# Gate and up of the second feed-forward block: eight partial products against seven, batch outside

## The reference, cut to what matters

```
def _L1_ffn_ref(x, w_gate, w_up, w_down):
    gate = jnp.einsum('bsd,hd->bsh', x, w_gate)      # 512 -> 2048
    up = jnp.einsum('bsd,hd->bsh', x, w_up)          # 512 -> 2048
    gated = jax.nn.silu(gate) * up
    return jnp.einsum('bsh,dh->bsd', gated, w_down)  # 2048 -> 512
...
x = x + 0.5 * _L1_ffn_ref(_layernorm(x), ...)
```

## Time and profile before

| | |
|---|---|
| runs | 2634.18, 2636.2, 2642.79 us |
| profiled execution: span from first to last instruction | 2632.3 us |
| TensorE busy | 2535.4 us (96%), mean granted clock 0.992 |
| VectorE / ScalarE / GpSimd busy | 1533.2 (58%) / 1035.6 (39%) / 981.6 us (37%) |
| chain that ended last, by engine | PE 81%, DVE 6%, POOL 2%, ACT 2%, SPq 2% |

### The profile page before, as it was taken

One profiled execution on the slowest core, in us unless ns is written; L12 is line 12 of the kernel. 1 busy time (PEld: TensorE's weight loads), 2 busy tenths in 40 slices (PEclk: granted clock), 3 DMA queues, 4 the chain that ended last, 5 costly groups with the idle time before them and its releaser, 6 DMA issues.

```text
span 2632.3 us, 44135 instructions
## 1 busy us (share of the span) xinstructions
PE 2535.4 (96%) x16928; PEld 2013.0 (76%) x16928; DVE 1533.2 (58%) x3356; ACT 1035.6 (39%) x1885; POOL 981.6 (37%) x1373
## 2 busy tenths in 40 slices
PE   6999989999999999999999999999999999999999
PEld 4788867667668888888888878677776678888887
DVE  7777579979975445433333345798589643333333
ACT  6555346656653223311111133566466431111111
POOL 5333566666643225211111122666366521111110
PEclk9999989999999999999999999999999999999999
DMA  4222131222220110100000002343233100000001
GB/s 148 73 73 73 39 76 46 51 68 64 48 93 1 36 45 12 37 25 25 24 25 25 25 17 58 92 94 75 52 88 79 37 32 25 24 25 25 25 17 64
DMA packets 72002, 128.73 MB, mean 49 GB/s; under 512 B 15728, under 2 KB 24944, under 8 KB 71792
## 3 DMA queue, kind: packets, MB, share of 16 engines
q1 hardware_dynamic: 71792, 125.92, 17.3%
HBM read 62.42 MB, written 13.63 MB: 29 GB/s over the span
## 4 chain that ended last, share of the span: by engine, by line
PE 81%; DVE 6%; POOL 2%; ACT 2%; SPq 2%; issue 2%; DMA 1%; DVEq 0%; ACTq 0%; POOLq 0%
PE psum L1049 65%; PE psum L1167 5%; PE psum L1130 4%; PE psum L1148 4%; PE psum L1178 2%; DVE psum L1501 2%; SPq L1745 1%; PE psum L1058 1%; DVE s1a0rden L1540 1%; ACT s1a0e L1335 1%; SPq L1764 0%; POOL s1a0e L1671 0%; ACT s4a1e L1335 0%; PE psum L1137 0%; POOL rstd L1610 0%
## 5 line engine op out<-in xcount | busy, mean ns | idle before, releaser
L1501 DVE CUSTOM_DVE_ANT_0 psum<-psum,mask_q 128x512 f32<-128x512 f32 (+5 forms) x768 | 413.2, 574 | 101.2 <-PE psum L1130 97.3
L1049 PE MATMUL psum<-hA_hi,wmem 128*128 128x256 f32 (+1 forms) x1536 | 405.2, 334 | 0.5 <-DVE s1a0negmax L1501 0.3
L1049 PEld LDWEIGHTS psum<-hA_hi,wmem 128*128 128x128 f32 x1536 | 270.3, 190 | 31.8 <-DVE s1a0negmax L1501 1.5
L1049 PE MATMUL psum<-hA_lo,wmem 128*128 128x512 f32 (+1 forms) x864 | 293.8, 340 | 0.0
L1335 ACT ACTIVATE s4a1e<-psum,p_scale 128x384 f32<-128x384 f32 (+5 forms) x384 | 205.5, 581 | 95.2 <-PE psum L1148 91.8
L1335 ACT ACTIVATE s1a0e<-psum,p_scale 128x384 f32<-128x384 f32 (+5 forms) x384 | 202.4, 578 | 78.1 <-PE psum L1148 76.8
L1454 DVE SCALAR_TENSOR_TENSOR x<-psum,x 128x512 f32<-128x512 f32 x256 | 175.7, 689 | 97.4 <-PE psum L1049 93.9
L1425 DVE TENSOR_TENSOR s5f1prod<-psum,s5f1silu 128x512 f32<-128x512 f32 x64 | 44.2, 691 | 303.7 <-PE psum L1049 303.7
L1425 DVE TENSOR_TENSOR s3f1prod<-psum,s3f1silu 128x512 f32<-128x512 f32 x64 | 44.2, 691 | 294.2 <-PE psum L1049 294.2
L1635 POOL TENSOR_TENSOR wmem<-raw,wmem 128x512 fp32r<-128x512 f32 x58 | 74.3, 1290 | 315.7 <-ACT wmem L1237 315.7
L1049 PE MATMUL psum<-s3f1w,s3f1a 128*128 128x512 f32 x768 | 181.6, 390 | 0.9 <-POOL s3f1w L1635 0.9
(11 more groups left out here) (195 smaller groups left out, 5581.8 us busy)
## 6 DMA issues: line engine op xcount, KB each, us to landing
s1a0qst<-s1a0qs SPq DMA_DIRECT2D x96, 128.0 KB, 2.3
s4a1qst<-s4a1qs SPq DMA_DIRECT2D x96, 128.0 KB, 2.4
s4a1kst<-s4a1ks SPq DMA_DIRECT2D x96, 128.0 KB, 2.4
raw<-in_gate SPq DMA_DIRECT2D x44, 256.0 KB, 2.9
raw<-in_up SPq DMA_DIRECT2D x44, 256.0 KB, 2.8
raw<-in_down SPq DMA_DIRECT2D x44, 256.0 KB, 2.8
rounded<-s0f0w SPq DMA_DIRECT2D x24, 256.0 KB, 2.0
s2f0w<-rounded SPq DMA_DIRECT2D x24, 256.0 KB, 4.9
```

The costliest lines, as they stand in the source:

```text
L1049: ins = pe.matmul(out_, w, m, start=n == 0, stop=n == len(terms) - 1)
L1501: dve.tensor_tensor_reduce(scores, scores, mask_q[:, first:first + pw], -1.0, -MASKED, ALU.add, ALU.min, T[s]["negmax"][n % 2][:, column:c ...
```

## The change

For f1 the chunk loop is replaced by rounds. A round is one batch (1024 tokens) and one group of 256 hidden columns; 16 rounds are a stage, batch outside, so that every weight group is loaded and split twice. In a round, gate and up are each one product of a 256 x 512 weight block with a 512 x 1024 block of LN output, both cut in 2 x 2. The eight half-depth products are replaced by Winograd's seven (`mul`, i = 0 to 6): 128 hidden columns, depth 256, 512 tokens, 6 matmuls each. They use seven combinations of weight blocks (sums by GpSimd, `g_sum`, split by `g_hi` on ScalarE and `g_lo` on GpSimd) and seven of the LN output, once per batch (`f_copy` on ScalarE and `f_sub` on VectorE per tile, split by `h_hi` and `h_lo`).

Products 0, 2, 4 and 5 accumulate in one PSUM bank, and 3 and 6 in another; product 1 has its own. After products 0, 2 and 4 the partial sum is copied out (`snap`: the gate's by ScalarE, up's by VectorE) before the next product may go on in the bank. VectorE adds copy and bank (`sum`). Then silu, multiplication (`gated`), `ahi`, `alo` as before, and `fold` is the old `down`. A round is 14 `mul` and 8 `fold`, 132 matmuls of 128x512. Round r's folds stand in round r+1.

`TURNS`, `AFTER_TURN` and the rest order this. Core of the diff:

```diff
+OPENS = {0: 0, 1: 1, 2: 0, 3: 3, 4: 0, 5: 0, 6: 3}
+SNAPS = (0, 2, 4)
+
+OUTS = ((0, 0, 1, 0), (1, 1, 3, 4), (1, 0, 5, None), (0, 1, 6, 2))
...
+FOLDS_AT = (2, 3, 4, 5, 6, 8, 9, 10)
+EARLY_TURNS = 8
...
+            for j in turns if r == 0 else range(len(TURNS)):
+                plan.extend(turn(s, r, j))
+                norms.tick(1 if j % 7 == 0 else 0)
+                weights.tick(int(j in (4, 5) or j > DOWN_AT[-1]))
...
+            def mul(s, r, n, i):
...
+                copied = {2: 0, 4: 2, 5: 4}.get(i)
+                if copied is not None:
+                    on.wait_ge(*copy_done(s, r, n, copied))
+                if i == 6:
+                    on.wait_ge(sem["sum"], at("sum", "sum", s, r, n, 1))
+                on.wait_ge(sem["g_lo"], at("g_lo", "g_lo", s, r, n, i))
+                on.wait_ge(sem["h_lo"], at("h_lo", "h_lo", s, r // GROUPS["f1"], i))
+                w = [by_half(part) for part in T[s]["block"][n][i]]
+                h = T[s]["h"][i]
+                terms = [(w[wp][:, k, :], h[hp][:, k, :]) for k in range(2) for wp, hp in THREE]
+                for k, (left, right) in enumerate(terms):
+                    ins = pe.matmul(psum[:, bank, :], left, right, start=OPENS[i] == i and k == 0,
+                                    stop=k == len(terms) - 1, skip_group_check=True)
...
+                dve.tensor_tensor(t1, bank[:, 0:2, :], b11, ALU.subtract).then_inc(sem["f_t1"], 1)
+                dve.tensor_tensor(t3, b22, bank[:, 0:2, :], ALU.subtract).then_inc(sem["f_t3"], 1)
...
+                dve.tensor_tensor(t2, bank[:, 2:4, :], t1, ALU.subtract).then_inc(sem["f_t2"], 1)
...
+                dve.tensor_tensor(t4, b21, t2, ALU.subtract).then_inc(sem["f_t4"], 1)
...
+                on.wait_ge(sem["mul"], at("mul", "mul", s, r, n, i))
+                dve.tensor_copy(T[s]["snap"][n][i == 2][:], psum[:, banks["mul", s, r, n, 0][0], :]).then_inc(sem["snap_up"], 1)
...
+                dve.tensor_tensor(buf[:], psum[:, banks["mul", s, r, n, OPENS[i]][0], :],
+                                  T[s]["snap"][n][copied == 2][:], ALU.add).then_inc(sem["sum"], 1)
...
+                pool.tensor_tensor(sums[:, 0], a21, a22, ALU.add).then_inc(sem["g_s1"], 1)
+                pool.tensor_tensor(sums[:, 2], a11, a21, ALU.subtract).then_inc(sem["g_s3"], 1)
...
+                pool.tensor_tensor(sums[:, 1], sums[:, 0], a11, ALU.subtract).then_inc(sem["g_s2"], 1)
...
+                pool.tensor_tensor(sums[:, 3], a12, sums[:, 1], ALU.subtract).then_inc(sem["g_s4"], 1)
```

More of the change, by code:

```diff
@@ L141, in make_plan, with norm_steps, norm @@
     last_norm, last_weight = {}, {}
[L143 to L146, removed]
+    def norm_steps(s, t):
+        kinds = ["ln_stats", "ln_norm", "ln_tp"]
+        if not by_rounds(s):
+            kinds += ["ln_hi", "ln_lo"]
+        else:
+            kinds += ["f_copy"] + ["f_sub"] * (t // CT % 2)
+        return [(kind, s, t) for kind in kinds]
+    def norm(s, c, into=0):
+        jobs = []
+        for t in range(c * CT, (c + 1) * CT):
+            steps = norm_steps(s, t)
+            wait = [[]] * (by_rounds(s) or by_rounds(s - 1)) * into
+            jobs.append([[steps[0]], *wait, [steps[1]], *wait, *wait, steps[2:]])
         last_norm[s, c] = jobs[-1]
@@ L175, in first_products @@
     def first_products(s):
+        if by_rounds(s):
+            steps = [[("begin", s)] + h_split(s, 0, 2)]
+            turns = [turn(s, 0, j) for j in range(EARLY_TURNS)]
+            return steps + [sum(turns[j:j + 2], []) for j in range(0, EARLY_TURNS, 2)]
         mts = MTS[STAGES[s]]
@@ L340, in attention @@
         put(jobs, last + 2, (UNITS - 4) // len(jobs))
+        if by_rounds(s + 1):
+            for i, at in enumerate(H_EARLY_AT):
+                put([[[step] for step in h_split(s + 1, 0, i)]], last + at, 0)
         if grouped:
@@ L421 @@
     "gu": ("gate", "up", "silu", "prod", "a_hi"), "a_lo": ("a_lo",),
+    "f_copy": ("f_copy",), "f_sub": ("f_t1", "f_t3", "f_t2", "f_t4"), "h_hi": ("h_hi",),
+    "h_lo": ("h_lo",), "g_sum": ("g_s1", "g_s3", "g_s2", "g_s4"), "g_hi": ("g_hi",),
+    "g_lo": ("g_lo",), "mul": ("mul",), "sum": ("sum",), "silu": ("silu_q",),
+    "gated": ("gated",), "ahi": ("ahi",), "alo": ("alo",), "fold": ("fold", "x_add"),
     "k_ones": ("k_ones",),
@@ L435, in raised @@
     if kind == "down":
-        return ("down", "dso", "x_pool") if STAGES[step[1]] == "f0" else ("down", "x_add")
+        return "down", "dso", "x_pool"
+    if kind == "snap":
+        return (("snap",), ("snap_up",))[step[3]]
     if kind == "v_out":
@@ L593, in run, with emptied_by @@
         return done[step]
+def emptied_by(s, r, n, i):
+    if i:
+        return "sum", s, r, n, OUT_OF[i]
+    return "silu" if n == GATE else "gated", s, r, OUT_OF[i]
 def bank_turns(plan):
@@ L867, in w_read @@
             p = s - 1
+            if by_rounds(s) and name == "down":
+                return [(sem["fold"], at("fold", "fold", s, g - 1, ST - 1))] if g else []
             if is_ffn(s):
@@ L1572, in vector_program @@
                      "q8": q8_, "q_b": q_b, "gu": gu, "a_lo": a_lo, "down": down,
+                     "f_sub": f_sub, "h_lo": h_lo, "snap": snap, "sum": sum_, "gated": gated_, "alo": alo, "fold": fold,
                      "turned": turned, "row": row, "row_min": row_min, "m_lo": m_lo, "v_out": v_out,
```

568 lines of the change are left out of this document (482 added, 86 removed).

## The result

The changed kernel took 2565.12 us (median of 4 runs, 2560.02 to 2569.59) against 2636.89 for the kernel before: ratio 0.9722, 95% interval 0.9703 to 0.9742. Its profiled execution took 2567.41 us with a span of 2565.7, against the 2552.2 that the sum gave; 66.6 us went where 80.1 were forecast. The median is 9.0 us over the forecast's 2556.1. The time lies in the stated range and the forecast's direction held; 13.5 us between the two profiled executions are to be accounted for. Ratios leave out two executions in a slower state, one of the kernel before (4170 us) and one of experiment 6 (5720 us).

What follows compares the result with a forecast made beforehand. TensorE's matmul count was taken to bound the f1 stages. Terms -87.2 + 1 + 8.7 - 6.6 + 3 + 0 + 1 = -80.1 took the 2632.3 us span to 2552.2; plus 3.9, 2556.1 us; own range 2546 to 2568, stretched for rivals to 2541 to 2588.

Steps and rivals of the forecast that it cites:

- The bound and the count: Both f1 stages: only the number of matmuls counts, 2304 a stage before and 2112 after, 384 fewer in two stages.
- The price of a matmul: f1 bodies: 0.2272 us each, from 32.71 us for 144 matmuls, so 384 fewer give -87.2 us.
- Added work in a round: Per 30.0 us round: VectorE 17.3, ScalarE 14.1, GpSimd 18.9 us, all under TensorE; +1 us for both stages' middle.
- a round over 30.5 us: Sign of being wrong: a round was to take 30.0 us from one first product to the next.
- Entry of s3: First round of s3: ScalarE and VectorE work exceeds TensorE's 19.1 us, so TensorE waits; +8.7 us, bounds 0 and 17.
- Entry of s5: Start of s5: 4 us lost where 10.6 were lost to waits and low clock; -6.6 us, bounds -10.6 to 0.
- Last group of s4: End of s4: GpSimd gets 6.6 us more work ahead of the exponentials' sums; +3 us, bounds 0 and 6.6.
- From s3 to s4: Stage boundary: LN work leaves it and the attention's first splits start 3 us later; 0, bounds -2 and +2.
- The lock between VectorE and GpSimd: First round of s3: two-SBUF-input VectorE instructions wait for GpSimd, some 2 us in all, 2558 for the sum.
- 1 (entries hide better): Rival: entries of s3 and s5 cost +1 and -8, all else +1; -93.4, 2543 us; chance 0.12.
- 2 (each round loses a product's time): Rival: a late copy or weight split costs 1.36 us every round, 44 us more, 2600; chance 0.15, milder or full.
- 3 (GpSimd the bound): Rival: GpSimd's queue bounds every round at 34.1 us, 45 over before, 2681 us; chance 0.03.

Runs made afterwards that it cites:

- experiment 6: Changed kernel with VectorE's low parts of token blocks done for one column only in the first batch of both f1 stages: 2551.04 us, ratio 0.9678.
- experiment 5: Changed kernel with product 1 of gate and up done twice in every round, giving back the 384 matmuls: 2644.27 us, ratio 1.0030.
- experiment 8: Changed kernel with ScalarE copying up's partial sums as well as the gate's: 2565.7 us, ratio 0.9732.
- experiment 2: Kernel before with feed-forward operand addresses aligned (64 bytes ahead of hA, 128 in s2): 2626.16 us, ratio 0.9956.
- Experiment 7: Changed kernel with GpSimd's low parts of weight blocks done for one column only in the first round of both f1 stages: 2559.41 us, ratio 0.971.
- experiments 1 and 3: Changed kernel with all feed-forward operands at the same address modulo 256: 2550.1 us; changed kernel with all f1 operands 192 bytes apart: 2574.82 us.

## Why the prediction was right, and where it was off

**The bound and the count.** Right. TensorE's waits are 0.3 us in the body of s3 and 1.6 in that of s5, experiment 5 prices 192 matmuls a stage at what they take once the entries are taken off, and experiment 8 shows that 3 x 0.69 us a round can move from VectorE to ScalarE without a change that can be told.

**The price of a matmul** is the term that was mis-sized most. At the measured means a body is 2304 x 0.2286 before and 2112 x 0.2310 after in s3, 2304 x 0.2285 and 2112 x 0.2297 in s5: 79.8 us in place of 87.2 (80.2 by these rounded means), a miss of 7.4. "The same multiplication two chunks later" was one sample in a kernel whose operands change place every two groups, and I carried it over to tiles that the change allots anew. The stretches of the earlier trace rows held a warning: 475.00 us for 2085 matmuls is 0.2278, and 488.00 for 2137 is 0.2284. At equal alignment the change is worth 2626.16 - 2550.1 = 76 us.

**Added work in a round.** The sizes are right where an instruction runs alone: copy 0.69, GpSimd 0.74. GpSimd was busy 63 to 67% of the bodies where 18.9 of 30.0 is 63%. VectorE was busier than forecast, 64 to 65% for 58%: its low parts (L1934) and those multiplications that read SBUF alone (L1927) took 0.88 us in the mean in s3 where 0.69 was put. The prediction had called the instructions with two SBUF inputs too few to matter; for the time they were, since VectorE was not the bound. It also named a round over 30.5 us as a sign of being wrong. From one round's first fold to the next one's it is 30.47 us in s3 with no other work, but 31.4 in the eight rounds of s3 that hold eight transposes of the LN each.

**Entry of s3**, forecast +8.7. The start held (1049.14 for 1049.1), and the waits for blocks came to 7.8 us, with the one for `g_lo`, where the steps of the prediction add up to 8.4. Not counted were the half clock behind the last of them, 3.4 us that cost 1.7, and the down split's 2.0. In all 1.25 + 7.8 + 1.7 + 2.0 - 0.9 = 11.9. I had seen at s5 of before that the clock was down after a wait of 3.75 us, and did not carry it to the waits that I was adding.

**Entry of s5**, forecast -6.6. The waits foreseen as 2.7 and 1.3 us were 2.35 and 2.23; the down split (1.3) and the clock (1.7) came on top: 7.6 lost for 10.6, so -3.0.

**Last group of s4**, forecast +3: from the first exponential of s4 to the last it took 2.0 us longer. That is all of s4, and in experiment 2, which leaves s4's steps as before, the same stretch took 4.5 us more than before, so the +2 is not shown to come from the last group. **From s3 to s4**, forecast 0: the last fold of s3 and the first exponential of s4 are 28.0 and 28.1 us earlier than before, 0.

**The sum** of the misses: 7.4 + 3.2 + 3.6 - 1.0 = 13.2 of 13.5 us. That it comes so close is in part luck. Cut at stage boundaries, the 66.6 us are 28.0 up to s3's last fold, -3.7 from there to s5's first product, and 42.3 in s5, and the terms above miss these by 1 to 2 us each, in both directions. Part of the 13.5 is also the pair of executions: wherever both are on record a time is about 1.7 us over its span, so the span of 2632.3 goes with a time of some 2634.0, next to the fastest run of the kernel before, while the changed kernel's profiled time is 2.3 over its median. The 3.9 us that the prediction added to the span were in part this. By the medians 71.8 us went. The rivals' list holds one slip of 0.2: -87.2 + 1 - 8 + 1 is -93.2, not -93.4.

**The lock between VectorE and GpSimd.** A token block's split (L1894), with two SBUF inputs, in the changed kernel (ns min/median/max):

```profile
L1894 DVE TENSOR_TENSOR s3f1h<-s3f1f,s3f1h x14: 1211/1462/2252, 1047.0 to 1304.1; 128x1024 fp32r<-128x1024 f32 x14
```

Half of them take 0.25 us or more over the shortest and the longest 1.04. The two that no GpSimd operation overlaps take 1.21 and 1.22. The longest, 2.25, begins while one of GpSimd's additions to x (L2154) has 1.17 us to run. Being held up beside GpSimd is as the Trainium skill (SBUF — State Buffer, section "SBUF: two separate sides") has it. What the first round would be without the lock no run shows. Experiment 7 took much of GpSimd's work out and its s3 was 3.0 us shorter, but the seven splits of its first batch still took 11.3 us in sum, against 11.5, so the gain is not from the lock on them.

**Rivals.** 1 (entries hide better) was wrong at both ends. 2 (each round loses a product's time) has its sign, since a round takes 30.5 us, but not its mechanism: hardly anything waits in the body. 3 (GpSimd the bound) is wrong for the rounds behind the first. In s3's first round GpSimd is busy 28.73 of 32 us and the chain of waits runs through it, but it is not the bound there by itself: with 14 of its operations out (experiment 7) s3 gained 3.0 us, and with VectorE's seven splits of token blocks out (6) 4.6.

## What to carry to other kernels

Take a matmul's price from the count over the whole body, by operand pair, not from one pair of rows; an engine that is busy 100% can still be 3% slow. When a change moves tiles, compare the operands' start addresses; 64 bytes in the right place and three other gaps gave 15 us here (12 of them in the two f1 stages), for no instruction. And look at a stage's first round as a chain through all queues: the engine named in a wait had itself been idle for two others, and a wait that is added can have the clock's price behind it: 1.7 us behind the one of 2.44 us in s3, nothing behind the one of 2.23 in s5.

## What the runs showed of the hardware that was not expected

A 128x512 fp32r matmul follows the last one after 0.2267 to 0.2275 us when its two operands start at the same address modulo 256 bytes, after 0.229 when the moving one is 64 above the stationary one, and after 0.2325 to 0.2335 at 128 or 192, in groups of 6 and of 24 alike. The value at 64 rests on one pair of addresses, 192 and 128. Where groups at different offsets alternate, those at 0 are slowed too (0.2306 for the folds of s3, 0.2271 once all are aligned). Two kinds do not follow: the output projection of attention keeps 0.2325 to 0.2335 at a difference of 0, and the value projection of s4 has 0.2287 to 0.2296 at 0 in the changed kernel and experiments 1 and 3. Why is open, as is what lies behind the offsets; differences that are not multiples of 64 were not tried.
